# Value projection in units of 128 tokens by 512 columns, in quads, with one buffer of split weights, on one Trainium2 core

## The reference

```
q = (layernorm(x) @ Wq); k = (ctx @ Wk); v = (ctx @ Wv)        # 2048x512 @ 512x4096 each
score = q k^T / sqrt(128) + bias, masked; probs = softmax(score)
x = x + tanh(g_xattn) * ((probs v) @ Wo)
x = x + tanh(g_ffn) * sparse_ffn(layernorm(x))                 # picks one of 32 rows per block
```

## Time and profile before

| | |
|---|---|
| median of 3 runs | 1855.76 us (1855.43 to 1855.97) |
| span of the profiled execution, first to last instruction | 1854.3 us |
| TensorE busy | 1840.5 us (99%) |
| VectorE busy | 1074.6 us (58%) |
| GpSimd busy | 957.8 us (52%) |
| ScalarE busy | 695.5 us (38%) |

### The profile page before, as it was taken

The page is one execution under the profiler, slowest core; times in us unless marked ns, Lnnn a source line. Parts: engine busy times, 40 slices in busy tenths (PEclk is TensorE's granted clock), DMA queues, the critical chain, the costliest instruction groups (busy, mean ns, idle before and its releaser), DMA issues.

```text
span 1854.3 us, 37953 instructions
## 1 busy us (share of the span) xinstructions
PE 1840.5 (99%) x15324; PEld 1587.8 (86%) x15324; DVE 1074.6 (58%) x1754; ACT 695.5 (38%) x1773; POOL 957.8 (52%) x758
## 2 busy tenths in 40 slices
PE   9999999999999999999999999999999999999999
PEld 8899988899998888888878888878888888888887
DVE  5443466433345455333447676786766886777663
ACT  4333243322223333333346555555555522222221
POOL 5767688666668888778735333343343121111110
PEclk9999999999999999999999999999999999999999
DMA  5555566644455555457658878798787650000000
GB/s 182 195 175 175 185 193 210 204 159 144 155 175 185 193 185 173 170 199 248 231 201 347 350 270 331 306 368 335 277 323 303 243 209 24 23 28 25 23 12 17
DMA packets 129693, 359.51 MB, mean 194 GB/s; under 512 B 12016, under 2 KB 53360, under 8 KB 118512
## 3 DMA queue, kind: packets, MB, share of 16 engines
q1 hardware_dynamic: 129520, 357.09, 53.7%
HBM read 229.11 MB, written 127.93 MB: 193 GB/s over the span
## 4 chain that ended last, share of the span: by engine, by line
PE 96%; DVE 2%; DMA 1%; POOL 1%; ACT 1%; issue 0%; SPq 0%; DVEq 0%; ACTq 0%
PE bank L1471 28%; PE bank L1473 28%; PE bank L1472 28%; PE bank L1574 4%; PE bank L1538 3%; PE bank L1554 2%; PE bank L1695 1%; PE bank L1672 1%; POOL wv_s_lo L732 0%; DMA ln_x<-in_x 0%; PE bank L1651 0%; DMA raw_tokens_first<-in_ctx_t 0%; PE bank L1638 0%; POOL wkq_lo L732 0%; ACT wv_s_hi L837 0%
## 5 line engine op out<-in xcount | busy, mean ns | idle before, releaser
L1471 PE MATMUL bank<-tokens_hi,wkq_hi 128*128 128x512 f32 x888 | 346.8, 391 | 1.2 <-DVE u L1089 1.0
L732 POOL TENSOR_TENSOR wkq_lo<-raw_wkq,wkq_hi 128x768 fp32r<-128x768 f32 x126 | 283.4, 2271 | 122.0 <-ACT wkq_hi L837 121.8
L1473 PE MATMUL bank<-tokens_hi,wkq_lo 128*128 128x512 f32 x888 | 345.6, 389 | 0.0
L1472 PE MATMUL bank<-tokens_lo,wkq_hi 128*128 128x512 f32 x888 | 345.6, 389 | 0.0
L1471 PE MATMUL bank<-wv_s_hi,tokens_hi 128*128 128x256 f32 x896 | 254.4, 284 | 0.7 <-POOL wv_s_lo L732 0.7
L1473 PE MATMUL bank<-wv_s_hi,tokens_lo 128*128 128x256 f32 x896 | 253.5, 283 | 0.0
L1472 PE MATMUL bank<-wv_s_lo,tokens_hi 128*128 128x256 f32 x896 | 253.5, 283 | 0.0
L1471 PE MATMUL bank<-wo_hi,attn_t_hi 128*128 128x512 f32 x512 | 205.7, 402 | 1.2 <-DVE attn_t_lo L1251 1.2
L1473 PE MATMUL bank<-wo_hi,attn_t_lo 128*128 128x512 f32 x512 | 199.9, 390 | 1.4 <-issue 1.4
L1472 PE MATMUL bank<-wo_lo,attn_t_hi 128*128 128x512 f32 x512 | 199.3, 389 | 0.5 <-issue 0.5
L1471 PEld LDWEIGHTS bank<-tokens_hi,wkq_hi 128*128 128x128 f32 x888 | 166.7, 188 | 36.3 <-DVE u L1089 1.4
(11 more groups left out here) (150 smaller groups left out, 3697.3 us busy)
## 6 DMA issues: line engine op xcount, KB each, us to landing
k_t<-c SPq DMA_DIRECT2D x128, 256.0 KB, 2.4
v_by_token<-c SPq DMA_DIRECT2D x128, 256.0 KB, 2.3
q_t<-c SPq DMA_DIRECT2D x128, 256.0 KB, 2.4
kt<-k_t SPq DMA_DIRECT2D x16, 2048.0 KB, 9.5
qt<-q_t SPq DMA_DIRECT2D x16, 2048.0 KB, 13.8
v<-v_by_token SPq DMA_DIRECT2D x16, 2048.0 KB, 12.4
raw_wkq<-in_wk SPq DMA_DIRECT2D x32, 512.0 KB, 4.1
raw_wv<-in_wv SPq DMA_DIRECT2D x16, 1024.0 KB, 5.9
```

What stands on the lines that cost most here:

```text
L732: pool.tensor_tensor(lo, job_raw(r)[:, a:b, :], hi.bitcast(F32), ALU.subtract)\
L1471: pe.matmul(o, a[0], b[0], start=first_mm, stop=False, skip_group_check=not grouped)
L1472: pe.matmul(o, a[0], b[1], start=False, stop=False, skip_group_check=not grouped)
L1473: return pe.matmul(o, a[1], b[0], start=False, stop=last_mm, skip_group_check=not grouped)
```

## The change

- A v unit is now one group of 128 tokens against 512 weight columns: 6 matmuls of 512 columns per product, 42 in all. There are still 32 of them. The same 512 columns serve four units, a quad.
- A quad needs two jobs of raw v weights (`V_JOB`, two to a quad), written side by side in one buffer per half; there is no second buffer, so ScalarE's high part 0 waits for the last product of the quad before.
- The order of units is four or three k units, then quads of v with two k units between them: quads start at units 4, 10, 16 and 22, and at 35, 41, 47 and 53.
- VectorE makes the low part 1 of all v jobs (`weight_lo`, `LO_DVE`), and the sums of every second v job and of both first ones of a half (`BY_DVE`).
- The token sets' steps are three units apart in place of five (`SET_STEPS`), and sets 1 and 2 start at units 26 and 57 in place of 22 and 52. The second sub-block's load stands in the same unit as its first sums, where it stood one unit ahead.
- k and q raw weights have memory of their own, and the arena is 222 KB in place of 207 KB. v is stored and loaded in rows of 512 floats.

```diff
+QUAD = 4
+def with_quads(half, first):
+    out, u = [("k", half, k) for k in range(first)], first
+    for quad in range(4):
+        out += [("v", half, QUAD * quad + t) for t in range(QUAD)]
+        more = 2 if quad < 3 else 16 - u
+        out += [("k", half, k) for k in range(u, u + more)]
+        u += more
+    return out
+UNITS = (with_quads(0, 4) + with_quads(1, 3) +
          [("q", 0, u) for u in range(16)] + [("q", 1, u) for u in range(16)])
...
-V_UNITS = [n for n, u in enumerate(UNITS) if u[0] == "v" and u[2] % 2 == 0]
+V_UNITS = [n for n, u in enumerate(UNITS) if u[0] == "v" and u[2] % QUAD == 0 for _ in range(2)]
...
-BY_DVE = [JOB_OF[V_UNITS[0]], JOB_OF[V_UNITS[8]]]
+def job_at(r):   # load, sums, part 0, part 1
+    f, is_v, i = JOBS[r]
+    if not is_v:
+        if any(UNITS[f - k][0] == "v" for k in (1, 2)):
+            return f - 4, f - 4, f - 3, f - 3
+        return f - 2, f - 2, f - 1, f - 1
+    if i % 8 < 2:
+        return f - 2 - i % 2, f - 2, f - 2, f - 1
+    return f - 5, f - 4 + i % 2, f - 2, f - 1
+BY_DVE = sorted((r for r in V_JOB if JOBS[r][2] % 2 or JOBS[r][2] % 8 == 0), key=lambda r: (job_at(r)[1], r))
+LO_DVE = [(r, part) for r, part in HI_ORDER if part and r in V_JOB]
...
-SET_FROM = {1: 22, 2: 52, 3: 64}
+SET_FROM = {1: V_END[0], 2: V_END[1], 3: 64}
+SET_STEPS = 3
...
-        vw = [[[at(f"wv_s{i}{j}_{n}", [P, 7, 2, 256], F32R, kb + 28 * j + 14 * k)
-                for k, n in enumerate(("hi", "lo"))] for j in range(2)] for i, kb in enumerate((60, 4))]
+        vw = [[at(f"wv_s{i}_{n}", [P, 7, 2, 512], F32R, kb + 28 * k) for k, n in enumerate(("hi", "lo"))]
+              for i, kb in enumerate((60, 4))]
...
             if i % 8 >= 2:
-                return pe_p[3], V_UNITS[i - 2] + 2
+                return pe_p[3], V_UNITS[i - 2] + QUAD
...
-                    if n == n0 + 4:
+                    if n == n0 + SET_STEPS:
                         sp.wait_ge(dve_xlo, token_part(i, 0, 2))
                         load_tokens(i, 1)
...
+            def weight_lo(r):
+                dve.wait_ge(*hi_part_done(r, 1))
+                hi, lo = (t[:, 3:7, :, :] for t in job_dest(r))
+                dve.tensor_tensor(lo, job_raw(r)[:, 4:8, :].rearrange("p a (c w) -> p a c w", c=2),
+                                  hi.bitcast(F32), ALU.subtract).then_inc(dve_wlo, 1)
...
                 for q in BY_DVE:
-                    if job_at(q)[0] == n - 1:
+                    if job_at(q)[1] == n - 1:
                         weight_sums(q)
                 sum_u2(n)
                 sum_u3(n)
                 token_step(n, 1)
+                for r, part in LO_DVE:
+                    if job_at(r)[2 + part] == n:
+                        weight_lo(r)
...
                 if kind == "v":
-                    for t in range(2):
-                        cols = slice((2 * (u % 2) + t) * P, (2 * (u % 2) + t + 1) * P)
-                        for c in range(2):
-                            mm = three(o[:, t * 256:(t + 1) * 256], hi_lo(tokens, full, XI[m], c, cols),
-                                       hi_lo(weights, full, WI[m], c, full),
-                                       first_of_bank and t == 0 and c == 0, c == 1, False)
+                    cols = slice(u % QUAD * P, (u % QUAD + 1) * P)
+                    for c in range(2):
+                        mm = three(o[:, :], hi_lo(tokens, full, XI[m], c, cols), hi_lo(weights, full, WI[m], c, full),
+                                   first_of_bank and c == 0, c == 1, False)
```

More of the change, by code:

```diff
@@ L194, in build @@
         vraw = [at("raw_wv0", [P, 8, 512], F32, 144), at("raw_wv1", [P, 8, 512], F32, 160)]
-        kraw = [at(f"raw_wkq{i}", [P, 8, 256], F32, 160 + 8 * i) for i in range(2)]
+        kraw = [at(f"raw_wkq{i}", [P, 8, 256], F32, 206 + 8 * i) for i in range(2)]
         o_c = {c: [at(f"{c}_{i}", [P, TB], F32, 176 + 4 * k + 2 * i) for i in range(2)]
@@ L203, in build @@
         lnxo = at("ln_xn_t", [P, CH, P], F32, 204)
-        mask_in = [at(f"mask_in{i}", [P, PPH, 2, S], U8, (206, 205)[i]) for i in range(HALVES)]
+        mask_in = [at(f"mask_in{i}", [P, PPH, 2, S], U8, (160, 205)[i]) for i in range(HALVES)]
         mask_rows = at("mask_by_row", [P, PAIRS, S], U8, 204)
@@ L373, in job_dest @@
             _, is_v, i = JOBS[r]
-            return vw[i // 8][i % 2] if is_v else kw[i % 2]
+            if is_v:
+                return [t[:, :, :, i % 2 * 256:(i % 2 + 1) * 256] for t in vw[i // 8]]
+            return [t[:, :, :, :] for t in kw[i % 2]]
         def job_raw_in(r):
@@ L450, in load_weights @@
                 kind, half, u = UNITS[f]
-                if r >= 2:
-                    prior = r - 1 if not is_v and JOBS[r - 1][1] else r - 2
-                    sp.wait_ge(pool_wlo, weight_part(prior, 1))
+                if i >= 2:
+                    prior = V_JOB[i - 2] if is_v else KQ_JOB[KQ_UNITS[i - 2]]
+                    sp.wait_ge(*lo_part_done(prior, 0))
+                    sp.wait_ge(*lo_part_done(prior, 1))
                 if is_v:
@@ L774, in _ @@
                 for r in range(2, len(JOBS)):
-                    _, a, b = job_at(r)
-                    if a == n:
-                        lo_part(r, 0)
-                    if b == n:
-                        lo_part(r, 1)
+                    for part in range(2):
+                        if job_at(r)[2 + part] == n and (r, part) in LO_POOL:
+                            lo_part(r, part)
                 t, late = divmod(n - LN_AT, 2)
@@ L782, in _ @@
                     do_rstd(t)
-                for r in range(2, len(JOBS)):
-                    if job_at(r)[0] == n and r not in BY_DVE:
+                for r in BY_POOL:
+                    if job_at(r)[1] == n:
                         sums(r)
@@ L914, in _ @@
                 for i, n0 in SET_FROM.items():
-                    sub, k = divmod(n - n0, 5)
-                    if 0 <= sub < 2 and k < 3:
+                    sub, k = divmod(n - n0, SET_STEPS)
+                    if 0 <= sub < 2:
                         token_hi(i, sub, k)
                 for r in range(2, len(JOBS)):
-                    _, a, b = job_at(r)
-                    if a == n:
-                        hi_part(r, 0)
-                    if b == n:
-                        hi_part(r, 1)
+                    for part in range(2):
+                        if job_at(r)[2 + part] == n:
+                            hi_part(r, part)
                 if n == NU - 1:
@@ L1480, in product @@
                 i = SET_OF[kind, half]
-                job = JOB_OF[n] if n in JOB_OF else JOB_OF[n - 1]
+                if kind == "v":
+                    half_jobs = V_JOB[8 * half + 2 * (u // QUAD):8 * half + 2 * (u // QUAD) + 2]
+                    parts_of = half_jobs if u % QUAD == 0 else []
+                else:
+                    parts_of = [KQ_JOB[n]]
                 o = bank[{1: n % 2, 2: n % 2, 6: 2, 7: 3 + n % 2, 4: 3 + n % 2, 5: 5 + n % 2, 3: 5 + n % 2}[m]]
                 first_of_bank = m in (1, 5, 6, 7)
-                tokens, weights = xs[i % 2], job_dest(job)
+                tokens, weights = xs[i % 2], vw[half] if kind == "v" else kw[KQ_UNITS.index(n) % 2]
                 if n == PLAIN:
@@ L1489, in product @@
                 if m == 1:
-                    pe.wait_ge(pool_wlo, weight_part(job, 0))
+                    for r in parts_of:
+                        pe.wait_ge(*lo_part_done(r, 0))
                     pe.wait_ge(act_c11, n - 1)
@@ L1494, in product @@
                 if m == 6:
-                    pe.wait_ge(pool_wlo, weight_part(job, 1))
+                    for r in parts_of:
+                        pe.wait_ge(*lo_part_done(r, 1))
                     if n == PLAIN:
@@ L1787, in blocks, with value_blocks @@
             .reshape(units, P, 4 * 2 * width)
+    def value_blocks(w):
+        w = w.reshape(2, 2, P, G // 2, 2, 2, 256)
+        order = [(1, 0), (0, 0), (0, 1), (1, 1)]
+        return np.stack([w[k, :, :, :, i, :, :].transpose(2, 3, 1, 0, 4) for i, k in order], axis=3)\
+            .reshape(G, P, 4 * 2 * 256)
     gates = np.concatenate([np.broadcast_to(a["g_xattn"].reshape(1, 1), (P, 1)),
```

93 lines of the change are left out of this document (52 added, 41 removed).

## The result

| | before | after |
|---|---|---|
| time, median of 4 runs each (us) | 1855.81 (1855.43 to 1855.97) | 1924.98 (1923.48 to 1925.61) |
| span of the profiled execution (us) | 1854.3 | 1923.8 |
| mean granted TensorE clock | 1.000 | 0.983 |

The changed kernel takes 1.0368 times as long (95% interval 1.0355 to 1.0380), 69 us more. The forecast was 1913 us, with a range of 1864 to 1928. Direction and mechanism held, and most terms of the sum did. Two were too small: the token loads by 5 us and the clock by 4.

What follows compares the result with a forecast made beforehand. TensorE's instructions, 96% of the chain of waits, were taken to bound the kernel. Span: 1854.3 - 18.9 + 39.0 + 15.2 + 6.7 + 15.3 = 1911.6 us, so 1913 us measured, range 1864 to 1928.

Steps and rivals of the forecast that it cites:

- token loads: Second sub-block's load issued in the unit needing it; next k unit's product 1 waits three times, 6.7 us in all.
- width and the old wait: 32 v units go from 10.08 to 9.52 us, and a 1.0 us u3 wait goes: 18.9 us gained.
- six later quads: Units f-2 and f-1 (f: quad's first unit): u3 waits of 6.8 or 5.9 us, c22 0.3 late; 39.0 us.
- first quads, less what the clock swallows: Units 3 and 34: waits for u3 and c22, 15.2 us, less 4.7 that a slower TensorE does not meet.
- lower clock: After eight waits of 3.5 to 7 us TensorE restarts at half pace, 2.5 us each: 20 us, 15.3 net.
- Turns: VectorE and GpSimd instructions with two SBUF operands alternate strictly, delaying v sums and u3; with clock loss, chance 0.50.
- VectorE keeps its turn: Rival: GpSimd enters only when VectorE's back-to-back row of instructions is through; 1858 us, chance 0.13.
- no blocking: Rival: VectorE and GpSimd do not block each other, sums cost only their own time; 1853 us, chance 0.08.
- VectorE's low part of 2048 elements: Two between u3 and c22 in unit f-1 (f: quad's first unit), taken as 2.3 us each.
- the clock does not fall: Rival: TensorE's waits bring no lower clock afterwards; 1898 us, chance 0.23.
- The Trainium skill's spacing: Rival: isolated matmuls spaced N/2.4 + 2.5 ns, so wider v units gain only 3.5 us; 1927 us, chance 0.06.

Runs made afterwards that it cites:

- Experiment 1: Changed kernel with VectorE's four sums of every second v job moved one unit earlier, to where GpSimd has no v low parts: 1872.57 us, ratio 1.0087.
- experiment 7: Changed kernel with GpSimd's v low parts 0 replaced by a copy of the raw block, one operand instead of two: 1884.48 us, ratio 1.0148.
- second run of the kernel after: Changed kernel measured once more without any edit, on the same chip as experiment 9: 1922.75 us, ratio 1.0360.
- experiment 9: Changed kernel with 24 extra matmuls that nothing reads ahead of product 4 in units 39, 45 and 51: 1916.1 us, ratio 1.0328.
- experiment 10: v products in two 256-column halves again, on the changed kernel with earlier second-block sums, early second token loads and first quads' work spread: 1864.6 us, ratio 1.0046.

## Why the prediction was right, and which terms were small

Point by point, with the sum's terms in us of span:

| step | forecast | measured in the profile |
|---|---|---|
| width and the old wait | -18.9 | -18.3 (16 x 0.56 + 16 x 0.52, and 1.0) |
| six later quads | 39.0 | 37.8 (3 x 6.59 + 3 x (5.67 + 0.35)) |
| first quads, less what the clock swallows | 15.2 - 4.7 | 12.6 (8.4 in unit 3, 4.2 in unit 34) |
| token loads | 6.7 | 11.8 (4.57, 2.86, 3.69; 0.7 behind them) |
| second stage | 0 | 1.7 (scores wait 2.8 for 1.1) |
| lower clock | 20.0 | about 24 (what remains; eleven low stretches) |
| span | 1911.6 | 1923.8 |

- **Turns.** Right in detail: sums of 4 us between GpSimd's low parts, six waits within 0.25 us of 6.8 and 5.9, and only 0.35 us for c22 in the second half. Experiment 1 removes the meeting and with it the waits; experiment 7 shortens GpSimd's instruction and with it the wait by exactly its share. The rivals "VectorE keeps its turn" and "no blocking" are out. One reading on which the step rested was wrong: the layernorm's instruction at 287.99 in the earlier trace rows has one operand of 512 elements in SBUF, ln_x, besides the mean and the deviation of each token, and not two. It took 2.07 us there and 0.54 at 326.46, so this row alone does not show that it takes two such operands; experiments 1 and 7 show the hold for sums that have two.
- **VectorE's low part of 2048 elements**, which no row had: 2.28 us each (4.48 for two), where 2.3 was taken.
- **First quads.** In unit 3 a part was missed: raw_wv lands later than assumed (7.2 us after its issue; the earlier trace rows had 6.5 for tokens of that size), ScalarE sits on it with TensorE's p1 copy queued behind, and TensorE waits 2.0 us for p1 before it waits for u3. ScalarE's row:

```profile
44.19 2.86 ACT L877 ACTIVATE wv_s_hi<-raw_wv 128x1536 fp32r<-128x1536 f32 x2 [5.16 <-DMA raw_wv<-in_wv]
46.95 0.58 ACT L909 ACTIVATE c<-bank 128x512 f32<-128x512 f32 x1
47.43 0.59 ACT L903 ACTIVATE p<-bank 128x512 f32<-128x512 f32 x1
```

- **Token loads: the place was right, the size too small, 6.7 against 11.8.** This is the largest miss of a term. I took the issue at T+1.56 from a step of the kernel before, and 6.5 us to landing. In unit 29 TensorE goes on from the unit before at T = 332.4 (its c21 comes 1.2 us later than usual, so T can't be read from it here). SyncE stood behind a k weights' load first:

```profile
334.74 2.33 SPq L504 DMA_DIRECT2D raw_wkq<-in_wk  x1
337.12 0.43 SPq L513 DMA_DIRECT2D raw_tokens<-in_ctx_t  x1
...
343.47 1.06 ACT L895 ACTIVATE tokens_hi<-raw_tokens 128x1024 fp32r<-128x1024 f32 x1 [9.12 <-DMA raw_tokens<-in_ctx_t]
```

  The load was issued at T+4.7, landed 6.3 us later, and TensorE went on at T+14.9. Issuing the weights' load took 2.33 us here; in the second run of the kernel after it took 0.41, and the wait was 3.2 us. At the other two places the issue came at T+1.6, as forecast, but the load landed 7.0 and 7.8 us after it (671.49 to 678.44, 742.72 to 750.51), and the waits were 2.9 and 3.7 us. So the late issue lengthened the first wait, and the slower landing the other two.
- **The clock: also mis-sized, 20.0 against about 24 us, or 15.3 against 19 when the 4.7 us that it was to swallow are taken off.** The figure is the difference of the spans less all else, so it carries the errors of the other rows. The trace agrees with it: over stretches of 1 us, TensorE's busy time multiplied by what its granted clock lacks to 1.00 sums to 22.8 us. The miss is in the count: the three token waits, 2.9 to 4.6 us long, brought a low stretch too, and I had counted eight, not eleven. The size of one was near the 2.5 us taken from the earlier trace rows: experiment 9 has about 2. The rival "the clock does not fall" is out.
- **Units.** The wider unit gives 0.52 to 0.56 us (experiment 10, 17.8 us in all). The Trainium skill's spacing (TensorE: Matmul & The Clock Gate, Back-to-back issue gap) would have made it an estimated 3.4 us in all (the prediction has 3.5); the measurement decides against it here.

## What to carry to other kernels

Before moving work between VectorE and GpSimd, list by unit which instructions with both operands in SBUF will be ready at the same time: here each GpSimd instruction that was ready between two neighbours cost VectorE its whole length, 3.8 us, and short sums in a row beside long instructions were the worst case. A wait of TensorE of several us is to be priced with the clock behind it (about 2 us each here), and work that only moves in time, as in experiment 1, can be worth more than the change itself (52 us against 18). The time to landing of a load that was hidden before isn't to be taken from one median: it was 6.3, 7.0 and 7.8 us at three places.

## What the runs showed of the hardware that was not expected

VectorE's instructions with one operand in PSUM are not held by GpSimd. In the kernel after, GpSimd is busy from 37.88 to 42.09 with two low parts, and c22 and c21 of unit 2 take their 0.69 us within that time:

```profile
39.34 0.69 DVE L1137 TENSOR_TENSOR c<-bank,u 128x512 f32<-128x512 f32 x1 [2.03 <-PE bank L1525]
40.70 0.69 DVE L1146 TENSOR_TENSOR c<-bank,u 128x512 f32<-128x512 f32 x1 [0.67 <-PE bank L1525]
...
37.88 4.21 POOL L775 TENSOR_TENSOR wkq_lo<-raw_wkq,wkq_hi 128x768 fp32r<-128x768 f32 x2
```

So u3, which reads PSUM too, is late because the held sums stand ahead of it in VectorE's queue. Sums put behind it should not delay it, but that was not tried by itself. The page of the Trainium skill cited at experiment 7 says that a VectorE instruction with at most one SBUF input, outside the two-port modes, does not contend with GpSimd; these two rows agree.

After the wait at 457.93 TensorE's clock did not come back with the work: it read 0.50 during 5.5 us of steady matmuls and only then 1.00. And the length of the wait alone did not decide whether it fell. In the second run of the kernel after, a wait of 2.46 us at 680 us brought a low stretch and one of 3.24 us at 348 us did not.
